# A fused attention and feed-forward kernel: value products grouped in two runs a pair, score maxima in other banks, result scaling at another place of the vector queue

## What is computed

```python
x  = L0_attn_x                                   # (8, 1024, 256)
xn = layernorm(layernorm(x)) * gamma
q, k, v = heads(xn @ Wq), heads(xn @ Wk), heads(xn @ Wv)
q = rotary(q) * 64 ** -0.5
kt = einsum('bhnd,hde->bhne', rotary(k), W_bilinear)
attn = softmax(einsum('bhid,bhjd->bhij', q, kt))
x = x + heads_back(attn @ v) @ Wo
x = x + feed_forward(layernorm(x))               # 256 -> 1024 -> gelu -> layernorm -> 256, ternary weights
```

## Time and profile before

| | us |
|---|---|
| runs of the kernel before, median of 3 | 3471.37 (3470.07 to 3475.37) |
| the profiled execution: time | 3466.45 |
| its span, first to last instruction | 3464.6 |
| mean granted TensorE clock of the span (share of 2.4 GHz) | 0.991 |

### The profile page before, as it was taken

One profiled execution on the slowest core, in us unless ns is written; L12 is line 12 of the kernel. 1 busy time (PEld: TensorE's weight loads), 2 busy tenths in 40 slices (PEclk: granted clock), 3 DMA queues, 4 the chain that ended last, 5 costly groups with the idle time before them and its releaser, 6 DMA issues. The chain is left out here.

```text
span 3464.6 us, 71914 instructions
## 1 busy us (share of the span) xinstructions
PE 3398.6 (98%) x21410; PEld 2200.6 (64%) x21410; DVE 2636.0 (76%) x4493; ACT 2313.3 (67%) x4412; POOL 2606.4 (75%) x1279
## 2 busy tenths in 40 slices
PE   6999999999999999999999999999999998899999
PEld 4655555555555555555555556566666664799998
DVE  6777777777777767777777777777777777899998
ACT  2666677666667766666766676677766666566665
POOL 2888888888889878888888888898888886122222
PEclk7999999999999999999999999999999999999999
DMA  5222323333323223332333333223322223333332
GB/s 197 83 88 95 119 94 102 102 123 102 102 92 117 98 98 102 118 102 96 99 123 102 102 102 119 96 94 100 118 90 93 75 74 113 101 100 100 102 105 69
DMA packets 255089, 355.75 MB, mean 103 GB/s; under 512 B 40220, under 2 KB 163484, under 8 KB 250268
## 3 DMA queue, kind: packets, MB, share of 16 engines
q1 hardware_dynamic: 245532, 343.29, 30.5%
q10 hardware_dynamic: 9216, 8.39, 0.7%
HBM read 219.49 MB, written 62.12 MB: 81 GB/s over the span
## 5 line engine op out<-in xcount | busy, mean ns | idle before, releaser
L463 POOL TENSOR_TENSOR prob_sum<-prob_sum,prob 128x1024 f32<-128x1024 f32 x762 | 1860.7, 2442 | 363.5 <-ACT prob L542 312.8
L542 ACT ACTIVATE prob<-scores 128x512 f32<-128x512 f32 x2048 | 1073.8, 600 | 525.8 <-PE scores L828 514.0
L752 DVE TENSOR_REDUCE row_max<-max_scores 128x1 f32<-128x512 f32 x1536 | 987.6, 684 | 428.0 <-PE max_scores L870 410.2
L1033 PE MATMUL attn_out<-prob,v 128*64 128x512 f32 x4096 | 934.3, 598 | 0.0
L819 PE MATMUL scores<-q_hi,k_hi 64*128 64x512 f32 x2048 | 785.5, 416 | 8.5 <-ACT prob L542 4.6
L824 PE MATMUL scores<-q_hi,k_lo 64*128 64x512 f32 x2048 | 755.5, 395 | 0.0
L828 PE MATMUL scores<-q_lo,k_hi 64*128 64x512 f32 x2048 | 751.8, 393 | 0.0
L1033 PEld LDWEIGHTS attn_out<-prob,v 128*64 128x64 f32 x4096 | 277.4, 137 | 565.3 <-issue 541.6
L870 PE MATMUL max_scores<-k_hi,q_hi 64*128 64x512 f32 x1536 | 578.9, 430 | 8.7 <-DVE row_max L752 5.5
L513 ACT ACTIVATE scores<-neg_max_seeds 128x512 f32<-128x512 f32 x1024 | 552.7, 598 | 42.7 <-DMA neg_max_seeds<-neg_max_halves 42.2
L819 PEld LDWEIGHTS scores<-q_hi,k_hi 64*128 64x128 f32 x2048 | 376.5, 185 | 284.0 <-issue 126.0
(11 more groups left out here) (148 smaller groups left out, 4771.9 us busy)
## 6 DMA issues: line engine op xcount, KB each, us to landing
rows<-rows SPq DMA_DIRECT2D x512, 128.0 KB, 2.0
neg_max_seeds<-neg_max_halves SPq DMA_DIRECT2D x128, 512.0 KB, 3.9
w_group<-w_parts SPq DMA_DIRECT2D x30, 1536.0 KB, 8.4
attn_normalised<-z_stage SPq DMA_DIRECT2D x128, 256.0 KB, 2.1
v<-attn_normalised SPq DMA_DIRECT2D x64, 512.0 KB, 4.1
sum_inverted_rows<-sums_inverted SPq DMA_DIRECT2D x126, 256.0 KB, 4.1
x_turned_parts<-x_tile_parts SPq DMA_DIRECT2D x49, 256.0 KB, 2.8
xt_batch<-x_turned_parts SPq DMA_DIRECT2D x7, 1792.0 KB, 10.3
```

The source lines that it names most:

```text
L463: nc.gpsimd.tensor_tensor(sums_of(k, half), a, prob[:, n % RING, :, :], ALU.add).then_inc(added, 1)
L542: nc.scalar.activation(prob[:, n % RING, e, :], S[e][n % 2][:, :], ACT.Exp).then_inc(exped[e], 1)
L752: nc.vector.reduce_max(mx[1 - u][:, e, n // 2, n % 2:n % 2 + 1], bank_of(e, jj)[:, :], axis=AX.X)\
L1033: nc.tensor.matmul(O[rows(e), :], V[k // 2 % 2][:, j, col:col + DH], prob[:, n % RING, e, :], start=j == 0, stop=j == 7).then_inc(pv_made[ ...
```

## The change

**Value products.** They no longer stand in every quad: the sixteen of q = 0 and q = 1 run together after the score block of q = 1, those of q = 2 and q = 3 after the keys of q = 3. Ahead of each run PE waits for a reduction of DVE, since bank O is now also used by maxima.

**Banks.** `bank_of` takes q: q = 0 and q = 2 keep X[0], X[1], M; q = 1 uses O, M, X[1], and q = 3 uses M, O, X[0]. The waits of the first three `max_score` of a quad and of the keys follow: in q = 3 the keys' first half (bank M) waits for the seventh reduction, where it had waited for the sixth.

**Moved.** On DVE `norm_z` goes from behind `rotate(Q)` to between the maxima of q = 0 and `rotate(K)`; `x_low` and `statistics` (the next batch's rows) go from q = 2 to q = 3, and the two copies that `x_low` needs do so on ACT. On SP the seeds and the column sums now stand ahead of the store of the results, and `store_x` behind `store_inverse`.

The diff, cut:

```diff
-        def bank_of(e, jj):
-            return (X[0], X[1], M)[MAX_ORDER.index((e, jj)) % 3]
+        def bank_of(e, jj, q):
+            return ((X[0], X[1], M), (O, M, X[1]), (X[0], X[1], M), (M, O, X[0]))[q][MAX_ORDER.index((e, jj)) % 3]
...
     # SP, span
+                if attn:
+                    max_seeds(t - 1, 1)
+                if k >= 1:
+                    sum_columns(t - 1)
                 if k >= 2:
                     for h in two:
                         store_z(k - 2, t - 2, h)
-                if k >= 1:
-                    sum_columns(t - 1)
-                if attn:
-                    max_seeds(t - 1, 1)
...
     # DVE, span
+                    if q == 0 and k >= 2:
+                        norm_z(k - 2, t - 2)
                     if q == 0:
                         if proj:
                             rotate(t, K)
...
                         if proj:
                             rotate(t, Q)
-                    if q == 0 and k >= 2:
-                        norm_z(k - 2, t - 2)
...
-                    if q == 2 and has_tile(k):
+                    if q == 3 and has_tile(k):
                         x_low(t, u)
-                    if q == 2 and has_tile(k + 1):
+                    if q == 3 and has_tile(k + 1):
                         statistics(t + 1, 1 - u)
...
     # PE, max_score (i is the place in MAX_ORDER)
+                elif q == 1:
+                    if i == 0:
+                        wait(pe, z_copied, 2 * t)
+                    elif i == 1:
+                        if proj:
+                            wait(pe, sin_made[Q], 2 * pp + 1)
...
+                    elif k >= 1:
+                        wait(pe, l_copied, t)
...
     # PE, span: keys
                                 if c == 0:
...
+                                    wait(pe, x_red[1], 16 * (t + 1) + 15)
+                                else:
                                     wait(pe, x_red[1], 16 * (t + 1) + 14)
-                                else:
-                                    wait(pe, x_red[1], 16 * (t + 1) + 15)
...
     # PE, span: value products
                         half = q // 2
-                        for jj in range(4):
-                            n = 4 * q + jj
+                        if q % 2 and prep:
+                            wait(pe, x_red[1], 16 * (t + 1) + (7 if q == 1 else 16))
+                        for n in range(8 * half, 8 * half + 8) if q % 2 else ():
                             j = n % 8
```

More of the change, by code:

```diff
@@ L403, in span @@
                     max_rows(t, 0)
-                if proj and has_tile(k) and p != PAIRS - 1:
-                    store_x(t, k, b)
                 if prep:
@@ L409, in span @@
                     store_inverse(t - 1)
+                if proj and has_tile(k) and p != PAIRS - 1:
+                    store_x(t, k, b)
                 if proj and p % 2 and k < T - 6:
@@ L576, in span @@
                                 nc.scalar.activation(wide[:, i, :], ones_full[:, :], ACT.Copy, scale=shift[:, i:i + 1]).then_inc(widened, 1)
+                    if q == 3 and has_tile(k):
+                        wait(act, x_turned, t + 3)
+                        wait(act, x_stored[u], 16 * ((t >> 1) + 1))
+                        for kt in range(KT):
+                            nc.scalar.activation(xparts[u][:, 0, kt, :], X[1][:, kt * P:(kt + 1) * P], ACT.Copy,
+                                                 scale=gam[:, kt:kt + 1]).then_inc(x_hi, 1)
                     if q == 3:
@@ L751, in span @@
                             wait(dve, x_made[e], 16 * (t + 1) + n + 1)
[L752 removed]
+                            nc.vector.reduce_max(mx[1 - u][:, e, n // 2, n % 2:n % 2 + 1], bank_of(e, jj, q)[:, :], axis=AX.X)\
                                 .then_inc(x_red[e], 1)
@@ L848, in max_score @@
                     wait(pe, lo_made[K], 2 * (t + 1) + 2)
[L849 to L868 removed]
+                elif q == 0:
+                    if i == 1:
+                        wait(pe, nm_hi, 2 * t + 1)
+                        if has_tile(k - 1):
+                            wait(pe, x_lo, 2 * (t + 2))
+                elif q == 1:
[5 more added lines that the diff above has]
+                        else:
+                            wait(pe, x_red[1], 16 * (t + 1) + 2)
+                    elif k >= 1:
+                        wait(pe, l_copied, t)
+                    elif attn:
+                        wait(pe, nm_hi, 2 * t + 2)
+                    else:
+                        wait(pe, x_red[1], 16 * (t + 1) + 4)
+                elif q == 2:
+                    if i == 0 and proj:
+                        wait(pe, sin_made[Q], 2 * pp + 2)
+                    else:
+                        wait(pe, x_red[1], 16 * (t + 1) + (3, 6, 8)[i])
+                elif i == 1:
+                    wait(pe, z_copied, 2 * t + 1)
+                elif proj:
+                    wait(pe, v_copied, 2 * pp + (1 if i == 0 else 2))
+                else:
+                    wait(pe, x_red[1], 16 * (t + 1) + (10 if i == 0 else 11))
@@ L869, in max_score @@
                 tile, part = n // 2, n % 2
-                nc.tensor.matmul(bank_of(e, jj)[:, :], QH[v][rows(e), tile * P:(tile + 1) * P], KH[v][rows(e), cols(part)],
+                nc.tensor.matmul(bank_of(e, jj, q)[:, :], QH[v][rows(e), tile * P:(tile + 1) * P], KH[v][rows(e), cols(part)],
                                  start=True, stop=True).then_inc(x_made[e], 1)
```

19 lines of the change are left out of this document (1 added, 18 removed).

## The result

| kernel | us, median (lowest to highest) | ratio to before, 95% interval |
|---|---|---|
| before, 4 runs | 3471.78 (3470.07 to 3475.37) | |
| after, 4 runs | 3763.43 (3758.04 to 3772.4) | 1.0841 [1.0815, 1.0867] |

The account below looks back on a forecast made before the run. PE was taken as the bound, busy for 3398.6 of 3464.6 us. Sixty pairs at 3.8 us plus 1.1 for the clock, 294 us, on the profiled 3466.45 gave 3760 us; range of 8 in 10: 3575 to 3880.

Parts of the forecast that it names:

- The last maxima: Values of q = 1 and keys of q = 3: PE waits 0.6 us each for the seventh reduction, 1.2 a pair.
- The gain: Grouped value products on PE: fewer changes of tile shape save 0.34 us a pair, 22 us over 64 pairs.
- The block of q = 1: PE's score block of q = 1: 4.56 us plus 0.6 of wait, from T + 9.9 to 15.05.
- The clock: PE idle from T + 3.1 to 5.9 lowers its granted clock: 1.1 us a pair, 66 us.
- the 228 us: Sixty pairs, each 3.8 us longer by norm_z's collision, waits for maxima and shape changes, without the clock loss.
- the 66: Loss by PE's lower clock after its idle time, 1.1 us a pair, in us.
- (b): Rival: norm_z ahead of K's rotation does not collide with POOL's additions; about 2.2 us a pair, 3596 us; chance 0.17.
- (c): Rival: each norm_z product waits one POOL addition more, full clock loss; 8.3 us a pair, 3964 us; chance 0.11.
- (d): Rival: norm_z fits a hole in DVE's wait, only waits for maxima remain; 0.9 us a pair, 3524 us; chance 0.07.
- (e): Rival: faster, only PE's shape changes matter, the seventh maximum's wait and norm_z being hidden; 3444 us; chance 0.03.

Follow-up runs that it names:

- z_early_only: The kernel before with only norm_z moved ahead of K's rotation; 3855.56 us, ratio 1.1120 to before.
- fill: The changed kernel plus ten 512-column matmuls that nothing reads, while PE waits for K's rotation; 3725.56 us, ratio 1.0734 to before.
- adds_small: The changed kernel with POOL's additions of the third and fourth tile of q = 0 on one column of each head; 3585.61 us, ratio 1.0326 to before.
- z_memset: The changed kernel with norm_z's products replaced by fills of one column without SBUF input; 3623.39 us, ratio 1.0453 to before.
- short_max: z_memset with maxima over 256 of 512 columns and the exponential's argument scaled by 0.01; 3563.62 us, ratio 1.0265 to before.
- z_back: The changed kernel with norm_z put back behind the rotation of Q; 3779.35 us, ratio 1.0894 to before.
- z_back_fill: z_back plus eight 512-column matmuls that nothing reads, behind the sums on PE; 3695.97 us, ratio 1.0653 to before.

## Why the prediction was right, step by step

**norm_z.** In the pair shown above, which is at the full clock, the steps came as predicted, the first seven within 0.2 us, the last 0.5 late: end of the products at T + 4.57 (4.6), K's rotation there at 5.8 (5.85), Q's projections 5.82 (5.9), q_lo 0.67 (0.7), sums 8.77 (8.9), scores of q = 1 9.77 (9.9), value run 15.23 (15.05), scores of q = 2 22.52 (22.05). Over 60 pairs, those at the lower clock included, the scores of q = 2 start at T + 23.1 in the mean, where they stood at 18.7 before: 4.4 us, with 3.3 and the clock's 1.1 forecast. The reasons stood in the earlier trace rows (such a product ends half a microsecond behind the addition) and in the earlier trace rows (when the additions can begin). The earlier trace rows alone would have misled: they show POOL where it is before the grouping, and z_early_only shows what that would have cost.

**The last maxima.** Predicted 0.6 before the keys and 0.6 before the values of q = 1. Measured 37.0 us over 63 pairs, 0.59 each, and 23.5 over 50, 0.47 each.

**The gain was mis-sized.** I took 0.34 us a pair: the whole difference between a block of 3.58 us and 16 x 0.2133. The runs of 32 matmuls take 7.09 us (median of 53, q = 1) and 7.00 (median of 52, q = 3) from start to start, where blocks of 3.58 + 3.58 and 3.58 + 3.53 stood: 0.18 us a pair, 11 us in all instead of 22. The 3.41 us of a block without its change of shape was the wrong part; products in this shape also pace at 0.22 us within a run (7.00 / 32), so only some 0.09 us of a block belong to the change of shape. The Trainium skill, "TensorEngine Tiling (Array Packing)", Key Properties, says that a change of the tiling mode drains TensorE. That there is a cost at each change agrees with these rows; that it is the drain, no run here shows.

**The block of q = 1** was taken as 4.56 us and 0.6 of wait. It takes 5.35 (median; mean 5.49, with 11.6 us in 15 waits of its maxima, L880, for DVE), and the run behind it 0.09 more than I had: 0.3 to 0.4 us a pair too little, some 20 us.

**The clock** was taken as 1.1 us a pair; fill won back 0.63, though it left 0.41 us of idle time and has its own matmuls. The stretches at half clock bound it at 53 us, 0.9 a pair. Some 30 us too much. So the total was right partly by luck: the 228 us were too low (by some 20 for the block of q = 1 and some 10 for the gain), the 66 too high by some 30, and they cancel.

**The rivals.** (b), norm_z without a collision, is adds_small: 3586 against 3596 forecast. (c), both products a whole addition each, is z_early_only: Q's projections at T + 7.5 (8.65 forecast), and 3856. (d) and (e) needed DVE to be free at a place where it isn't: even with norm_z gone, q_lo took over. What I had missed is that last point. For the change itself q_lo's 0.7 us was right; for the experiments I did not see that it is the other half of an exchange, and so z_memset and short_max came out 43 and 104 us above my theories. z_back came out 129 us above; 83 of these went with the fill, so with the lower clock, which I had put at next to nothing there; the rest I put down to the same exchange.

What stays open: whether another order of DVE's work around q = 1 would make the grouping pay; the gain of the grouping itself is some 11 us, and no run tried to save both collisions in a kernel that leaves nothing out.

## What to carry to other kernels

Before an instruction of DVE with two operands in SBUF is moved, lay POOL's timeline of the changed kernel beside its new place, not that of the kernel before: it may stand for up to one whole instruction of POOL, and if it doesn't, the next such instruction may. Products that look like cover with no use of their own (value products between two score blocks) hide another engine's work; gathering them saved 0.18 us a pair here and bared 1.1 us of waits for maxima; with the collision and the clock a pair got 4.7 us longer. Where an idle time of TensorE can't be removed, matmuls that nothing reads can pay: 38 us here, and 83 in z_back_fill.

## What the runs showed of the hardware

- A DVE instruction with two SBUF inputs on one column stood 1.90 us for an addition of POOL on 1024 columns, and took 0.15 us where it fell on the seam between two additions that depend on each other; two products on 512 columns took 3.5 us there.
- POOL is held up as well: two additions took 5.49 us instead of 4.88 around one product of 0.68 us.
- An idle time of TensorE of 2.70 us in each pair was followed by a granted clock of 0.5 in about half of the pairs (29 stretches, 106 us); one of 4.38 us in nearly all (59 stretches, 396 us); the 2.70 us with ten matmuls in them, in two pairs alone (6.8 us).
- One change of tile shape and back less saved 0.07 us (q = 1) and 0.11 us (q = 3) of TensorE's time.
